# The first thought ends one tile later, and the first group's preparation runs behind three gates

## The reference

```
x = x + 0.5 * ffn(layernorm(x), ...)
x = x + attn(layernorm(x), w_attn, w_o)
x = x + 0.5 * ffn(layernorm(x), ...)

def ffn(x, ...):                       # x: (2, 2048, 1024)
    x_norm = layer_norm(x, in_gamma, in_beta)
    thought = x_norm[:, -1, :] @ agg_w + agg_b        # the last token of each sequence alone
    for _ in range(4):
        t = layer_norm(thought, pn_gamma, pn_beta)
        t = gelu(t @ d1_w + d1_b)                     # 1024 -> 4096
        thought = thought + (t @ d2_w + d2_b)         # 4096 -> 1024
    broadcast = (thought @ bc_w + bc_b)[:, None, :]
    gate = sigmoid(x @ gate_w + gate_b)               # every token
    return layer_norm(x + gate * broadcast, out_gamma, out_beta)

def attn(x, w_attn, w_o):              # windows of 128 tokens, each sees itself and the one before
    q, k, v = split(x @ w_attn.T);  q = q / 128
    sim = where(keep, q @ k.T, 0);  out = square(relu(sim)) @ v
    return out @ w_o.T
```

## Time and profile before

| | us |
|---|---|
| median of three runs | 2033.42 (2031.25 to 2034.07) |
| the profiled execution | 2035.73 |
| its span, first to last instruction | 2034.5 |
| TensorE busy | 1958.1 |
| VectorE busy | 1262.6 |
| ScalarE busy | 696.5 |

### The profile page before, as it was taken

One profiled execution on the slowest core, in us unless ns is written; L12 is line 12 of the kernel. 1 busy time (PEld: TensorE's weight loads), 2 busy tenths in 40 slices (PEclk: granted clock), 3 DMA queues, 4 the chain that ended last, 5 costly groups with the idle time before them and its releaser, 6 DMA issues.

```text
span 2034.5 us, 31033 instructions
## 1 busy us (share of the span) xinstructions
PE 1958.1 (96%) x12136; PEld 1036.5 (51%) x12136; DVE 1262.6 (62%) x2286; ACT 696.5 (34%) x1025; POOL 169.5 (8%) x278
## 2 busy tenths in 40 slices
PE   7998999999999999999999999999999999999997
PEld 3333444344434447665665655566655664444443
DVE  2322687324343567678787757666566637888887
ACT  1578546213223332223333122221122213444442
POOL 0000011000000010010100000000000001111111
PEclk9999999999999999999999999999999999999999
DMA  9589997889999863369979899989989966555552
GB/s 366 204 329 370 336 337 261 318 306 368 370 362 377 311 229 107 104 222 288 335 261 335 308 311 309 352 295 309 362 269 307 349 234 184 156 155 156 151 150 73
DMA packets 275216, 555.80 MB, mean 273 GB/s; under 512 B 149040, under 2 KB 149248, under 8 KB 274688
## 3 DMA queue, kind: packets, MB, share of 16 engines
q1 hardware_dynamic: 275072, 553.83, 78.5%
HBM read 406.93 MB, written 113.26 MB: 256 GB/s over the span
## 4 chain that ended last, share of the span: by engine, by line
PE 57%; DMA 11%; DVE 9%; SPq 2%; issue 1%; ACT 1%; POOL 1%; DVEq 0%; ACTq 0%
PE product_banks L1101 45%; PE product_banks L1136 4%; DMA thought_units<-parts_scratch 3%; PE thought_acc L1300 3%; PE product_banks L1235 2%; PE thought_acc L1290 2%; DMA gate_arena<-arena 2%; DMA thought_units<-in_d_w 2%; DVE bn_parts L1537 2%; DMA arena<-gate_scratch 1%; DMA arena<-qk_scratch 1%; SPq L1022 1%; DVE thought_units L1936 1%; SPq L884 1%; DVE arena L1713 1%
## 5 line engine op out<-in xcount | busy, mean ns | idle before, releaser
L1101 PE MATMUL product_banks<-gate_arena,arena 128*128 128x512 f16 x1536 | 353.6, 385 | 0.0
L1101 PE MATMUL product_banks<-wide_a,thought_units 128*128 128x512 f16 x1536 | 331.7, 379 | 0.0
L1101 PE MATMUL product_banks<-gate_arena,wide_a 128*128 128x256 f16 x2688 | 306.4, 275 | 9.4 <-DMA gate_arena<-arena 9.4
L1101 PE MATMUL product_banks<-wide_b,gate_arena 128*128 128x512 f16 x1344 | 299.2, 379 | 0.0
L1101 PEld LDWEIGHTS product_banks<-gate_arena,wide_a 128*128 128x128 f16 x2688 | 262.8, 99 | 57.0 <-issue 23.5
L1101 PEld LDWEIGHTS product_banks<-gate_arena,arena 128*128 128x128 f16 x1536 | 149.0, 99 | 197.8 <-issue 40.9
L1101 PEld LDWEIGHTS product_banks<-wide_a,thought_units 128*128 128x128 f16 x1536 | 150.3, 98 | 181.2
L1101 PEld LDWEIGHTS product_banks<-wide_b,gate_arena 128*128 128x128 f16 x1344 | 129.4, 98 | 157.6 <-issue 11.3
L1537 DVE BATCH_NORM_STATS2 bn_parts<-arena 128x6 f32<-128x512 f32 x256 | 164.3, 684 | 4.5
L2000 POOL TENSOR_TENSOR token_stats<-stats,minus_half 128x1 f32<-128x1 f32 x96 | 67.5, 703 | 988.0 <-DVE stats L1545 814.6
L1562 DVE SCALAR_TENSOR_TENSOR arena<-product_banks,inverse_gate,arena 128x512 f32<-128x512 f32 x64 | 47.8, 749 | 139.4 <-PE product_banks L1101 129.5
(11 more groups left out here) (221 smaller groups left out, 2365.5 us busy)
## 6 DMA issues: line engine op xcount, KB each, us to landing
thought_units<-parts_scratch SPq DMA_DIRECT2D x275, 512.0 KB, 7.8
thought_units<-in_d_w SPq DMA_DIRECT2D x174, 512.0 KB, 7.0
arena<-in_x SPq DMA_DIRECT2D x64, 512.0 KB, 9.3
parts_scratch<-thought_units SPq DMA_DIRECT2D x64, 512.0 KB, 6.1
x_scratch<-arena SPq DMA_DIRECT2D x64, 512.0 KB, 8.9
thought_row<-in_d_w SPq DMA_DIRECT2D x50, 512.0 KB, 7.2
arena<-x_scratch SPq DMA_DIRECT2D x40, 512.0 KB, 7.4
gate_scratch<-arena SPq DMA_DIRECT2D x32, 512.0 KB, 8.2
```

The source lines that it names most:

```text
L1101: mm = pe.matmul(bank, left(i, k), right(j, k), start=(n == 0), stop=(n == 3 * KD - 1))
```

## The change

`LATE` is 3 instead of 4: the gates of tiles 12 to 28 instead of 12 to 27 carry the thought and the splits of the folds (these at the same pace as before, so at the same places against the gates), and tiles 29 to 31 stand behind it. The preparation of group 0 has one rest instead of two ahead of its second `prep_norm` and three instead of four behind, and is paced at 1.3 pieces per TensorE piece instead of 1.15. The gate saves are spread 3, 3, 2 over the three tiles in place of two after each of four.

```diff
-EARLY, LATE = 12, 4
+EARLY, LATE = 12, 3
...
-    prep = [("rest",)] * 2 + [("prep_norm", 1), ("prep_beta", 1)] + [("rest",)] * 4
+    prep = [("rest",)] + [("prep_norm", 1), ("prep_beta", 1)] + [("rest",)] * 3
     prep += [p for p in plan_prep(0) if p not in before]
     late = []
     for n in range(LATE):
-        late += plan_gate(TILES - LATE + n) + [("gate_save", k) for k in range(2 * n, 2 * n + 2)]
-    out += paced(late, prep, 1.15, PE_PIECES)
+        late += plan_gate(TILES - LATE + n) + [("gate_save", k) for k in range(3 * n, min(3 * n + 3, KD))]
+    out += paced(late, prep, 1.3, PE_PIECES)
```

## The result

| | before | changed |
|---|---|---|
| median, us (7 runs each) | 2032.98 (2025.26 to 2034.07) | 2019.95 (2014.74 to 2024.27) |
| profiled execution, us (its span) | 2035.73 (2034.5) | 2015.01 (2013.8) |

The ratio is 0.9938, with a 95% interval of 0.9918 to 0.9958. The changed kernel is 13 us faster. A second measurement of it on another chip gave 0.9936 (0.9917 to 0.9955) with a median of 2017.48. The two profiled executions are 20.7 us apart and overstate the difference. I forecast 2032.0, between 2025 and 2039.

What follows compares the result with a forecast made beforehand. It took TensorE, busy 1958.1 of 2034.5 us, to bound the kernel. Profiled 2035.7 + 0.6 (between the stages) - 2.0 (waits for weights) = 2034.3; on the median's scale 2033.4 - 1.4 = 2032.0 us, range 2025 to 2039.

Steps and rivals of the forecast that it cites:

- Part 1: Turn of tile 30, at 715.92: the 3.24 us wait and its low clock go, -4.9 us up to tile 31's end.
- Parts 2 to 4: End of stage 1: thought's row taken up about 720, second transpose 3.4 us later at 752.0, gates landing 1.1 us earlier.
- Part 5: Up to group 1's queries: VectorE's chain only 1.1 us earlier, TensorE waits 4 us, clock falls (1.7 us); 4.9 given back.
- the seam: Between stages 1 and 2, up to group 1's queries: -1.1 us for the chain, +1.7 for the clock, +0.6 in balance.
- Part 6: Stage 1, thought spaced 3.8% wider: -2.0 us from waits for weights; everything else 0, bounds -7.7 and +7.7.
- stage 1 is dealt anew: Rival: the wait at 561.53 vanishes with its clock (-7.7, about 2024; 0.09) or another comes up (about 2039.5; 0.09).

Runs made afterwards that it cites:

- c1: Kernel before with seven pieces of the first thought put by hand where the changed kernel has them, or about there; 0.9975.
- c2: Changed kernel with the same pieces, except those of the vo fold, and two high parts put back where the old kernel had them; 0.9983.
- f2: Changed kernel with the old kernel's order up to the end of the fold of vo (tiles 0 to 11); 0.9991 of the kernel before.
- a1: Changed kernel with the thought's steps spaced as in the kernel before, new end of stage 1 kept; 1.0000 of the kernel before.
- b4: Kernel before with the thought's steps spaced closer, 1.875 units instead of 1.95; 0.9960.
- d1: Changed kernel with the thought's steps spaced closest, 1.875 in place of 2.02; 0.9959 of the kernel before.
- a4: Kernel before with the first preparation steps moved later, so that the turn of tile 30 doesn't wait; 1.0002.

## Why the prediction was wrong

**Part 1, the stall, held.** No wait at the turn of tile 30. From the gates of tile 28 to the first values it is 44.8 us (689.82 to 734.65) against 48.3 (702.16 to 750.50): -3.5 us. In it are 0.8 us of lower clock behind the wait at 688.05 (8 matmuls in 2.67 us, where 1.90 is usual) and the thought's last matmuls, 215 in all against 211. With these taken off it is near the -4.9.

**Parts 2 to 4, the row, the preparation and SyncE's queue, held** within 2.2 us. The row is taken up at 708.82, which is 19.0 us after the gates of tile 28 begin (forecast: 720 on the old scale, 17.8 us). It is published 1.9 us after it is stored. SyncE in order of time, changed (start, us of issuing):

```profile
698.77 0.33 SPq L983 DMA_DIRECT2D row_scratch<-t_wide  x1
...
700.64 0.32 SPq L992 DMA_DIRECT2D thought_row<-row_scratch  x1
...
738.84 2.27 SPq L1022 DMA_TRANSPOSE thought_units<-arena  x1
...
742.39 0.86 SPq L1009 DMA_DIRECT2D arena<-gate_scratch  x1
```

The second transpose goes 4.2 us behind the end of the gates' matmuls, where I had 6.4. VectorE has its gates 14.7 us behind that end, where I had 15.5:

```profile
749.39 1.23 DVE L1691 TENSOR_TENSOR arena<-arena,thought_row 128x1024 f32<-128x1024 f32 x1 [10.24 <-DMA arena<-gate_scratch]
```

**Part 5, what is late next, held in the wait; its clock was a matter of chance.** TensorE waits 1.02 + 2.21 = 3.2 us, where I had 4, and the seam comes out at -0.5 us, where I had +0.6. In this profile the clock did not fall behind the wait of 2.21 us. In the second profile of the same kernel it did, behind a wait of the same 2.21 us, and there the seam is +1.4. Stretches of 8 us behind it, the first profile and then the second:

```profile
783.00:791.00 8.00, 7.16 (x54) 5.30 (x55) 5.62 (x11) 1.73 (x2) 1.46 (x2) 1.00 1.05 320
```

```profile
781.00:789.00 8.00, 7.63 (x43) 4.65 (x44) 4.47 (x10) 1.25 (x2) 0.33 (x1) 0.79 1.04 360
```

That the 4.9 us are given back is shown three times: by the two traces, by the kernel without the stall (1.0002) and by the new seam with the old spacing (1.0000).

**Part 6 is the step that failed.** It took the spacing at -2.0 us and "everything else between 60 and 700 us" at 0, with bounds of 7.7 to either side; it was some -13 us in the medians. The -2.0 for the loads was about right: the waits for weights came to 6.2 and 6.7 us in the changed kernel's two profiles, 9.3 before. (Its bound was not: three runs of loads at 1.9 us each give 5.7 us, not 4.8.) The 0 for everything else is what failed, and two things were wrong in it.

First, the size: the bound was the price of one wait, that of 4.28 us at 561.53, and its clock. But that was one of eight waits of 1 us or more for VectorE or ScalarE between 60 and 700 us, and a new order deals them all again. Before tile 12 alone five of them, 3.23, 1.41, 3.82, 3.20 and 2.52 us, each with 1.7 us of lower clock in or behind it, come to 22.7 us. A bound from one row can't hold a sum over five.

Second, the value: I took 0 because I did not look. The new order is known before any run, and so are VectorE's and ScalarE's queues at each of these waits. Whoever had asked of the five, one by one, whether the pieces that stand in front of the bank's release in the old trace still stand there in the new order, would have found three of them gone, and the 1.41 behind the first with it (c1 moves the pieces of the three by hand, c2 those of two of them, and f2 gives the effect of the whole order). That would have got the sign right, but not the size: the four are 11.0 us, with 6.8 of clock 17.8, and the stretch became only 11.7 us shorter. New waits, which can't be read off so easily, took the rest: 2.96 us where 1.04 stood, 1.97 where there was none, and 2.7 us for loads.

So the rival "stage 1 is dealt anew", which I gave 0.09 for faster at about 2024, was the case in kind, by other waits than the one that it names: the wait at 561.53 is gone, but one of 3.44 us at 549.06 has come up, and the gates of tiles 12 to 31 are no shorter (305.5 and 306.0 us, the latter with the 15 matmuls more). It should have been the leading one.

What is settled: the gain depends on the spacing (a1) and does not grow with its width (b4, d1), it is made by the order up to tile 11 (f2), and three places where the thought stood ahead of a bank's release carry a good part of it (c1, c2). What stays open: the 5 to 8 us of the first two parts that the single moves of c1 didn't bring, what keeps or loses the gain behind tile 12, and why stage 2, with one and the same order, took 936 to 949 us in these profiles.

## What to carry to other kernels

When a parameter spreads one stream of work over another, changing it deals out anew every place at which a piece of the one stands ahead of a bank's release in the other; the sum over these places can be larger than what the change is for, and of either sign. Take the list of the bottleneck's waits in the old trace, look up for each which instructions stood in front of the releaser, and look in the new order whether they still do; bound what is left by the sum of the waits of that kind, not by one, since new waits come up and take a part back. And if such a change wins, try the parameter at two or three other values: here the old value was a bad one, with better ones on both sides.

## What the runs showed of the hardware

The long waits for VectorE before tile 12 come back to within 0.3 us in every kernel that has the same order: in all six profiles with the old order up to tile 11 they are 3.23 us at 163 to 167, 3.8 to 4.1 at 264 to 269, 3.2 at 314 to 320 and 2.5 at 352 to 358. Waits for loads come back less well: that of 2.44 us at 667.48 was 1.70 and 1.75 us in two others with the same order (a1 and a4). What the clock makes of a wait does not come back, and the length of the wait doesn't decide it. The two profiles of the changed kernel differ behind the same 2.21 us, as shown above, and behind the same 2.96 us (1.00 over 6 us from 229, 0.80 over 8 us from 225.5). Of two kernels at the same place of the program, the changed one and then the version with moved pieces, the first waited 2.77 us and the second 3.53 us:

```profile
312.00:320.00 8.00, 7.43 (x33) 4.13 (x34) 5.30 (x10) 3.41 (x6) 0.00 (x0) 0.79 0.91 352
```

```profile
312.00:320.00 8.00, 7.71 (x42) 4.30 (x43) 6.73 (x15) 5.02 (x7) 0.00 (x0) 1.00 0.88 348
```

Behind the shorter wait the granted clock was 0.79 over 8 us (1.7 us lost, at the level of 1.2 GHz for part of it), behind the longer one 1.00, the level of 2.4. My rule in part 5, that a wait of 3.24 us brings the fall and one of 2.44 doesn't, was drawn from two rows and is wrong. These rows say that a clock fall belongs in a forecast as a chance, not as a term. The Trainium skill (TensorE: Matmul & The Clock Gate, Part 1: The HAM clock gate) says of the start of a kernel that one and the same kernel shows a different number of matmuls at the slow clock from run to run. The two profiles of the changed kernel agree with that in kind, but behind waits in its middle and not at its start.
